# Turned one-hots of the second edge stage: from broadcast rows by DVE instead of by PE and ACT

## What is computed

```python
h = (x_flat @ W_gat).reshape(M, HEADS, NUM_EXPERTS)
...
e = jax.nn.leaky_relu(a_src[src] + a_dst[dst], negative_slope=0.2)
e_max = jax.ops.segment_max(e, dst, num_segments=M)
ee = jnp.exp(e - e_max[dst])
denom = jax.ops.segment_sum(ee, dst, num_segments=M)
...
msg = h[src] * alpha[:, :, None]
agg = jax.ops.segment_sum(msg, dst, num_segments=M)
...
for ei in range(NUM_EXPERTS):
    hh = jax.nn.gelu(x @ W1[ei] + b1[ei], approximate=False)
    out = out + g[..., None] * (hh @ W2[ei] + b2[ei])
```

## Time and profile before

| what | us |
|---|---|
| median of 3 plain runs | 4171.85 (4165.95 to 4173.73) |
| span of the one profiled execution, which is its own time | 5269.4 |
| of it the first edge stage (143.6 to 3096) | 2952.4 |
| of it the second edge stage (3240 to 5127) | 1887.0 |
| PE busy over the span | 3476.8 (66%) |
| DVE busy over the span | 3039.4 (58%) |
| POOL busy over the span | 2649.1 (50%) |
| ACT busy over the span | 1492.7 (28%) |

### The profile page before, as it was taken

One profiled execution on the slowest core, in us unless ns is written; L12 is line 12 of the kernel. 1 busy time (PEld: TensorE's weight loads), 2 busy tenths in 40 slices (PEclk: granted clock), 3 DMA queues, 4 the chain that ended last, 5 costly groups with the idle time before them and its releaser, 6 DMA issues. The chain is left out here.

```text
span 5269.4 us, 87248 instructions
## 1 busy us (share of the span) xinstructions
PE 3476.8 (66%) x16727; PEld 2890.9 (55%) x16728; DVE 3039.4 (58%) x9074; ACT 1492.7 (28%) x4965; POOL 2649.1 (50%) x2767
## 2 busy tenths in 40 slices
PE   5555555665566665666655537888888888888860
PEld 4444444444454444444444436777777777777760
DVE  5566655555565666666666665555555555555558
ACT  3222222222222222222222213333333333333310
POOL 1555555555555555555555522555555555555540
PEclk9777777777777777777777766888888888888865
DMA  5322333332333333333332242111111111111118
GB/s 121 82 78 75 84 82 81 84 84 79 82 82 99 101 101 102 100 101 101 101 84 78 77 79 49 20 20 22 20 20 22 20 20 22 20 21 21 20 16 239
DMA packets 224394, 356.43 MB, mean 68 GB/s; under 512 B 65743, under 2 KB 143761, under 8 KB 224051
## 3 DMA queue, kind: packets, MB, share of 16 engines
q0 software_dynamic: 114560, 234.67, 19.2%
q1 hardware_dynamic: 100624, 109.13, 7.5%
q10 hardware_dynamic: 8867, 9.05, 0.6%
HBM read 294.17 MB, written 45.66 MB: 64 GB/s over the span
## 5 line engine op out<-in xcount | busy, mean ns | idle before, releaser
L791 POOL DMA_INDIRECT msg<-table,idx x1680 | 1630.7, 971 | 1305.1 <-ACT rel L806 844.6
L1466 POOL DMA_INDIRECT xmsg<-xtable,xidx x1060 | 1002.8, 946 | 889.0 <-ACT xidx L1482 589.7
L1159 PE MATMUL psS_e<-msg,hot 128*125 128x260 f32 x3360 | 1182.9, 513 | 281.4 <-issue 162.2
L1159 PEld LDWEIGHTS psS_e<-msg,hot 128*125 128x125 f32 x3360 | 815.5, 254 | 512.3 <-issue 337.3
L888 DVE TENSOR_TENSOR room<-room,psS_e 125x260 f32 x842 | 356.5, 423 | 361.7 <-remote 180.9
L1024 DVE TENSOR_TENSOR msg<-msg,psW_e 128x1024 f32<-128x1024 f32 x420 | 509.5, 1213 | 8.8 <-issue 1.1
L812 ACT CAST hotT<-psT_e 125x512 bf16<-125x512 f32 x422 | 244.7, 580 | 951.6 <-remote 649.7
L1012 DVE TENSOR_REDUCE look<-psD_e 128x32 f32<-128x96 f32 x420 | 106.6, 254 | 700.7 <-remote 553.8
L1076 PE MATMUL psD_e<-ad_b,hotT 125*128 x1684 | 133.9, 182 | 559.8 <-issue 151.3
L1655 PE MATMUL psY<-w,hid 128*125 128x256 f32 x1600 | 457.1, 447 | 56.7 <-issue 29.6
L1065 PEld LDWEIGHTS psT_e<-ident,hot 128*125 128x125 f32 x1692 | 320.7, 240 | 248.2 <-ACT hotT L812 157.7
(11 more groups left out here) (308 smaller groups left out, 4436.9 us busy)
## 6 DMA issues: line engine op xcount, KB each, us to landing
msg<-table,idx POOLq DMA_INDIRECT x1680
experts_out<-y_room SPq DMA_DIRECT2D x101, 224.0 KB
y_back<-experts_out SPq DMA_DIRECT2D x25, 896.0 KB
xmsg<-xtable,xidx POOLq DMA_INDIRECT x1060
xs<-x_all SPq DMA_DIRECT2D x100, 125.0 KB
table<-hrow SPq DMA_DIRECT2D x50, 113.8 KB
x_all<-in_x SPq DMA_DIRECT2D x5, 1120.0 KB
xin<-in_x SPq DMA_DIRECT2D x50, 112.0 KB
```

The source lines that it names most:

```text
L791: nc.gpsimd.indirect_dma_start(msg[:, u, j, :], None, table[:, :], bass.IndirectOffsetOnAxis(ap=idx[:, u, j:j + 1], axis=0)).then_inc(gath ...
L1159: last = nc.tensor.matmul(psS[:, u % 2, j // GT, 0:ROW], hot[:, u, j, :], msg[:, u, j, :], start=j % GT == 0, stop=j % GT == GT - 1)
L1466: nc.gpsimd.indirect_dma_start(msg[:, u, j, :], None, xtable[:, :], bass.IndirectOffsetOnAxis(ap=idx[:, u, j:j + 1], axis=0)).then_inc(gat ...
```

## The change

The turned one-hots are no longer made by PE and ACT. In `nodes`, PE turns the rows of all edges once (eight matmuls with a bfloat16 unit matrix), ACT copies them to SBUF, and one DMA stores them in DRAM as `lo_rows`, a line of 128 numbers for each group. In the second edge stage ACT's `stage`, now four steps ahead, copies the source numbers, copies the rows to float32 (`lo`), adds the class's start to the blocks (`hi_rel`), and issues a DMA that broadcasts the 512 rows of the step to all 128 partitions (`lo_bc`, bfloat16). DVE's `turned_hot` compares them with the partition's number, two steps ahead, and so writes `hotT` in bfloat16. The table of end scores is split once into three bfloat16 parts (`xad_b`); a pick gives 5 times 3 times 8 numbers per edge, and DVE's product and sum work on 480 instead of 160 numbers per partition. DVE's one-hots now read `lo` and `hi_rel`, so `one_hot` and `step` no longer fetch the step's place; the fetch in `add` stays. PE's `turn`, ACT's `keep_turned` and the PSUM tile between them are gone. The diff, cut to its core:

```diff
...
-XAHEAD = 3
+XAHEAD = 4
...
+    lo_rows = nc.dram_tensor("lo_rows", [XEP, P], BF16).ap()
...
     def row(v):
...
+        psL = ps("psL_n", [P, 2, 512])
+        ident_b = sb("ident_b", [P, P], BF16)
+        lo_turned = sb("lo_turned", [P, 2, 512], BF16)
...
+            nc.scalar.copy(ident_b[:], ident[:]).then_inc(ident_kept, 1)
+            for h in range(2):
+                act.wait_ge(los_turned, h + 1)
+                nc.scalar.copy(lo_turned[:, h, :], psL[:, h, :]).then_inc(los_kept, 1)
+            act.wait_ge(los_kept, 2)
+            act.dma_start(lo_rows.rearrange("(c r) e -> r c e", r=P),
+                          lo_turned[:].rearrange("p h (c e) -> p (h c) e", e=P)).then_inc(los_stored, 16)
...
+            act.wait_ge(los_stored, 16)
...
         @block.tensor
         def _(pe):
+            pe.wait_ge(ident_kept, 1)
+            los = lo_all[:].rearrange("p s j -> p (s j)")
+            for h in range(2):
+                for c in range(4):
+                    at = (h * 4 + c) * P
+                    last = nc.tensor.matmul(psL[:, h, c * P:(c + 1) * P], los[:, at:at + P], ident_b[:], start=True,
+                                            stop=True)
+                last.then_inc(los_turned, 1)
             def turn(n):
...
-    CF = CB * 2 * XH
+    XP = 3 * 2 * XH
+    CF = CB * XP
...
+        lo = sb("xlo", [P, XRING, XT])
+        hi_rel = sb("xhi_rel", [P, XRING, XT])
...
-        hotT = sb("xhotT", [NB, 3, XT, P])
+        hotT = sb("xhotT", [NB, 3, XT, P], BF16)
+        xad_b = sb("xad_b", [NB, BLOCKS, 3, 2 * XH], BF16)
+        lo_bc = sb("lo_bc", [P, XRING, XT * P], BF16)
+        rowid = sb("rowid", [P, 1])
...
-        prod = sb("xprod", [P, XT, CB, 2 * XH])
+        prod = sb("xprod", [P, XT, CB, XP])
...
-        psT = ps("psT_g", [NB, 512])
...
+        step_rows = lo_rows.rearrange("(s j) e -> s (j e)", j=XT)
...
         def _(pool):
...
+            nc.gpsimd.iota(rowid[:], [[0, 1]], base=0, channel_multiplier=1,
+                           allow_small_or_imprecise_dtypes=True).then_inc(iotas, 1)
...
             def stage(k, w):
...
-                nc.scalar.copy(idx[:, RING[w], :], xs_i[:, bass.ds(at, 1), :].rearrange("p a j -> p (a j)")) \
-                    .then_inc(staged, 1)
-            def keep_turned(k, w):
-                act.wait_ge(hot_turned, k + 1)
-                nc.scalar.copy(hotT[:, TURN[w], :, :], psT[:, 0:XT * P].rearrange("p (j e) -> p j e", j=XT)) \
-                    .then_inc(hotT_ready, 1)
+                nc.scalar.copy(idx[:, RING[w], :], xs_i[:, bass.ds(at, 1), :].rearrange("p a j -> p (a j)"))
+                nc.scalar.copy(lo[:, RING[w], :], lo_all[:, bass.ds(at, 1), :].rearrange("p a j -> p (a j)"))
+                nc.scalar.activation(hi_rel[:, RING[w], :], hi_all[:, bass.ds(at, 1), :].rearrange("p a j -> p (a j)"),
+                                     ACT.Identity, bias=cls_rel[:, bass.ds(k, 1)]).then_inc(staged, 1)
+                act.dma_start(lo_bc[:, RING[w], :], step_rows[bass.ds(at, 1), :].to_broadcast([P, XT * P])) \
+                    .then_inc(lo_loaded[RING[w]], 16)
...
             def step(k, w):
...
-                if exists(k, 2):
-                    keep_turned(*later(k, w, 2))
...
-            for a in range(2):
-                keep_turned(a, a)
...
         def _(dve):
...
-            dve.wait_ge(iotas, 1)
+            dve.wait_ge(iotas, 2)
...
+            left = prod[0:NB].rearrange("p j b f -> p (j b f)")[:, 0:BLOCKS * 2 * XH] \
+                .rearrange("p (b f) -> p b f", b=BLOCKS)
+            split = Chain(dve, xad_split)
+            split.link(V.tensor_copy(left, xad_all))
+            three_parts(nc, split, left, xad_b)
...
             def one_hot(k, w):
-                at = step_at(dve, k)
-                V.tensor_tensor(hot[:, RING[w], :, :], bcast(node_p, 1, XT),
-                                bcast(lo_all[:, bass.ds(at, 1), :].rearrange("p a j -> p (a j)"), 2, NB),
-                                ALU.is_equal).then_inc(hot_ready, 1)
+                dve.wait_ge(staged, k + 1)
+                V.tensor_tensor(hot[:, RING[w], :, :], bcast(node_p, 1, XT), bcast(lo[:, RING[w], :], 2, NB),
+                                ALU.is_equal)
+            def turned_hot(w, visit):
+                u = RING[w]
+                dve.wait_ge(lo_loaded[u], (visit * RING.count(u) + (w // XRING + 1)) * 16)
+                V.tensor_scalar(hotT[:, TURN[w]].rearrange("p j e -> p (j e)"), lo_bc[0:NB, u, :], rowid[0:NB], None,
+                                ALU.is_equal).then_inc(hotT_ready, 1)
...
             def step(k, w, visit, first):
...
-                at = step_at(dve, k)
...
-                blk = bcast(hi_all[:, bass.ds(at, 1), :].rearrange("p a j -> p (a j)"), 2, CB)
-                first_of = cls_rel[:, bass.ds(k, 1)]
-                ch.also(V.scalar_tensor_tensor(hi[:], blk, first_of, bcast(bid_p, 1, XT), ALU.add, ALU.is_equal))
+                blk = bcast(hi_rel[:, u, :], 2, CB)
+                ch.also(V.tensor_tensor(hi[:], bcast(bid_p, 1, XT), blk, ALU.is_equal))
...
-                ch.link(V.scalar_tensor_tensor(hi_p, blk, first_of, bcast(bid_p, 1, XT), ALU.add, ALU.is_equal))
+                ch.link(V.tensor_tensor(hi_p, bcast(bid_p, 1, XT), blk, ALU.is_equal))
...
-                                bcast(hi[:], 3, 2 * XH), ALU.mult).then_inc(picked_read, 1)
+                                bcast(hi[:], 3, XP), ALU.mult).then_inc(picked_read, 1)
...
-                ch.link(V.reduce_sum(look[:], prod[:].rearrange("p j b f -> p j f b"), AX_X))
+                ch.link(V.reduce_sum(look[:], prod[:].rearrange("p j b (s f) -> p j f (b s)", s=3), AX_X))
...
+                if exists(k, 2):
+                    turned_hot((w + 2) % SPAN, visit + (w + 2) // SPAN)
...
+            for a in range(2):
+                turned_hot(a, 0)
...
-            def turn(k, w):
-                pe.wait_ge(hot_ready, k + 1)
-                if not (isinstance(k, int) and k == 0):
-                    pe.wait_ge(hotT_ready, k)
-                for j in range(XT):
-                    last = nc.tensor.transpose(psT[:, j * P:(j + 1) * P], hot[:, RING[w], j, :], ident[:])
-                last.then_inc(hot_turned, 1)
             def pick(k, w):
...
-                                            xad_all[:, bass.ds(c * CB, CB), :].rearrange("p b f -> p (b f)"),
+                                            xad_b[:, bass.ds(c * CB, CB)].rearrange("p b s f -> p (b s f)"),
...
-            turn(0, 0)
-            turn(1, 1)
+            pe.wait_ge(xad_split, 6)
...
-            turn(2, 2)
...
             def step(k, w, i=None):
...
-                if exists(k, 3):
-                    turn(*later(k, w, 3))
...
```

More of the change, by code:

```diff
@@ L252, in build @@
             nodes(nc, scope, xmix, W_gat, xatt_src, xatt_dst, xtable, x_all, ident, agg, ex_self, xnT, hg_all, xad_all,
-                  row)
+                  lo_all, lo_rows, row)
         acc = sb("acc", [NB, BLOCKS, XROW])
         y_dram = nc.dram_tensor("experts_out", [XE * (BLOCKS // 2) + 1, NB, 2 * D], F32).ap()
-        gating_sums_and_experts(nc, scope, xs_i, lo_all, hi_all, step_i, cls_i, cls_rel, xtable, xad_all, W1, b1, W2, b2, ident, zeros,
+        gating_sums_and_experts(nc, scope, lo_rows, xs_i, lo_all, hi_all, step_i, cls_i, cls_rel, xtable, xad_all, W1, b1, W2, b2, ident, zeros,
                                 node, xnT, acc, y_dram, row)
@@ L1181, in _, with nodes @@
                             step(s, part, first, t, u)
-def nodes(nc, scope, xmix, W_gat, xatt_src, xatt_dst, xtable, x_all, ident, agg, ex_self, xnT_all, hg_all, xad_all, row):
+def nodes(nc, scope, xmix, W_gat, xatt_src, xatt_dst, xtable, x_all, ident, agg, ex_self, xnT_all, hg_all, xad_all,
+          lo_all, lo_rows, row):
     U = 2
@@ L1209, in nodes @@
         psG = ps("psG_n", [NB, U, 512])
+        psL = ps("psL_n", [P, 2, 512])
+        ident_b = sb("ident_b", [P, P], BF16)
+        lo_turned = sb("lo_turned", [P, 2, 512], BF16)
+        ident_kept = sem("ident_kept_n")
+        los_turned = sem("los_turned_n")
+        los_kept = sem("los_kept_n")
+        los_stored = sem("los_stored_n")
         loaded = sem("loaded_n")
@@ L1351, in _, with gating_sums_and_experts @@
                 mm.then_inc(projected, 1)
-def gating_sums_and_experts(nc, scope, xs_i, lo_all, hi_all, step_i, cls_i, cls_rel, xtable, xad_all, W1, b1, W2, b2, ident, zeros, node,
+def gating_sums_and_experts(nc, scope, lo_rows, xs_i, lo_all, hi_all, step_i, cls_i, cls_rel, xtable, xad_all, W1, b1, W2, b2, ident, zeros, node,
                             xnT, acc, y_dram, row):
@@ L1394, in gating_sums_and_experts @@
         iotas_kept = sem("iotas_kept")
+        xad_split = sem("xad_split")
         chain = sem("chain_g")
@@ L1398, in gating_sums_and_experts @@
         gathered = [sem(f"gathered_g{u}") for u in range(XRING)]
-        hot_ready = sem("hot_ready_g")
-        hot_turned = sem("hot_turned_g")
```

(1 more changed line is left out.)

## The result

The changed kernel takes 3974.34 us (median of 4 runs, 3972.2 to 3978.38), the kernel before 4170.0 us beside it: ratio 0.9528, interval 0.9515 to 0.9542. It is faster by 196 us; the forecast was 4120 us, and the result lies under the range (4035 to 4210).

The account below looks back on a forecast made before the run. In the second edge stage PE and DVE's chain were taken as so close that they hold each other up; 4172 + 21 (chain) + 2 (start) - (110 - 35) (waits) = 4120 us, range 4035 to 4210.

Parts of the forecast that it names:

- waits for PE and ACT: Second edge stage, DVE: of 110 us of waits in the plain run, 35 stay, so the time falls by 110 - 35.
- the sum of DVE's chain: Second edge stage, DVE per step: -0.66 - 0.53 + 0.33 + 0.57 + 0.37 = +0.08 us, +21 us over 265 steps.
- the 1497 us: DVE's chain in the second edge stage without its waits: 265 steps of 5.65 us, experts' additions and 25 loop turns included.
- the 110 us of waits: DVE's waits in the plain second edge stage, bracketed between 0 and 110 us; the upper end was taken.
- Fetches, product, sum: DVE per step: two fetches go, -0.66 - 0.53 us; product grows to 480 elements, +0.33; strided sum grows, +0.57.
- The compare: DVE's new 512-element compare: 0.45 us long from one-source rows, adding 0.37 us a step (0.21 to 0.60).
- DVE was the bound already: Rival, second edge stage: only 60 us of waits in the plain run, 35 staying, time 4170 us; chance 0.15.
- More waits in the plain run: Rival, second edge stage: half of the profiled 390 us, 195, is in the plain run, time 4035 us; chance 0.14.
- PE falls by 309 us (forecast 313): PE, second edge stage: without turning and with bfloat16 picks, work drops by 313 to 1119 us, under DVE's chain.
- not under 0.74: Sign of the clock rival: PE's granted clock under 0.74 makes PE the bound again; at 0.70, 4200 us; chance 0.07.
- ACT's late Exp: ACT ahead of DVE's weighing: two one-hots, about 1 us, cover the Exp; without that cover DVE waits up to 0.6 us.
- the compare waits for POOL: Rival, DVE's compare: it waits until POOL's running gather ends, 0.36 us a step, 95 us, time 4215 us; chance 0.13.

## Why the prediction was wrong

The direction was right, the mechanism and the size were not: -52 us forecast, -196 us measured. The forecast let DVE's chain grow a little and took its whole gain, 75 us, from waits for PE and ACT, because "PE and DVE's chain are so close that they must hold each other up". The runs show the reverse: the waits gave 24 us, and DVE's own order the rest. So the direction came out right partly by luck. The step that failed is the sum of DVE's chain, "+0.08 us a step", which measured -0.38, together with the 25 turns of the loop that were left inside the 1497 us as something that stays, and the 110 us of waits.

| term | forecast | measured | from |
|---|---|---|---|
| fetches, us a step | -1.19 | -1.22 | 6.00 - 4.78, fetches put back |
| form and reading place of the one-hots, us a step | 0 | -0.33 | 6.33 - 6.00, no staging against fetches put back |
| product, us a step | +0.33 | +0.33 | 0.36 to 0.69, start to start |
| sum, us a step | +0.57 | +0.58 | 0.47 to 1.05 |
| compare, us a step | +0.37 | +0.26 | its start to the next one's |
| together, times 265, us | +21 | -101 | 4.78 - 5.16 |
| turn of the loop, us | 0 | -73 | 24 times (4.13 - 0.79) - (0.47 - 0.18) |
| waits for PE and ACT, us | -75 | -24 | 58.6 to 34.5 |
| start, us | +2 | not told apart | |
| sum, us | -52 | -198 | |

*Fetches, product, sum.* Right to 0.03 us each; all three were read from single rows of the same kind.

*The other operands.* The prediction counted instructions that vanish and instructions that grow, and passed over two that only change their form: the one-hots of blocks lost the scalar that hangs on the step and a source at a fetched place (0.234 us in L1558 above, 0.172 in L1596), and the register work for their addresses went too. That is -0.33 us a step, 87 us, and the largest miss. Of it 0.19 us come with the class's start when the fetches are there (0.10 without them) and 0.14 with the reading place. The two instructions' own lengths make up 0.12 us; that the rest is register work is argued, not shown.

*The loop's turn.* Its gap was in the trace of before; it was never read, because only ordinary steps were. Taking the fetches' instructions out of the loop removed it, about 73 us. Not the fetch as such does it: covered, the two fetches cost no time in a step, and the gap was there.

*The compare.* Taken at 0.45 us from the one-source rows, it takes 0.345 us undisturbed. That is 29 us of the miss. Written in float32 it takes 0.478 us (median of the run with float32 picks), less than the 0.60 us that was the sign there of a length hanging on bfloat16 at both ends, and 0.133 us more than in bfloat16. The Trainium skill, "VectorE: DVE Perf Modes", section "The perf-mode tier table", gives four elements a cycle for bfloat16 and two for float32; the estimate from it, 0.29 us, was nearer to the 0.345 us than the 0.45 us taken. The compare into float32 reads bfloat16, a mix that the table doesn't list.

*The waits.* Taken at the upper end of their bracket, 110 us, because PE's rows came close to it; they were 58.6 us, and 34.5 stay. The rival "DVE was the bound already" had put 60 and 35 there, and was right on that; its time failed with the same chain. "More waits in the plain run" came nearest in time with the wrong mechanism.

*PE, ACT, DMA, clock.* PE falls by 309 us (forecast 313), near it partly by luck: the groups of the turning and the picks fell by 369 us, and the experts' second products took 53 us more. The granted clock is 0.90, not under 0.74, no DVE group waits for the broadcast rows, which land in 3.1 us, and ACT's late Exp costs 2.7 us. The errors that lowered the time (compare 29, form 87, loop 73 us) and the one that raised it (waits 51 us) don't cancel.

## What to carry to other kernels

When numbers move from a register-addressed table to a staged tile, count three things on the engine that is relieved: the exposed fetch, the form of every instruction that used the number, and the length of its loop. Look at the step where a loop turns as closely as at an ordinary one: a gap there that goes with the instruction packets was paid on 23 of 24 turns here. And try each part of a change alone, since here a part that costs 279 us by itself and one that gives 190 us by itself together gave 196.

## What the runs showed of the hardware

The strided sum of 480 numbers is 0.358 us quicker when they lie in PSUM (0.658 against 1.016 us). Before that run it was only a guess from the shorter sums of the earlier trace rows.

The rival "the compare waits for POOL" exists in small. In the changed kernel the compare takes 342 to 589 ns; over 1.2 times its median in 53 of 265 cases, 9.4 us together (9.9 us with a few smaller ones). These are all the compares that began 0.47 to 0.65 us after a gather's start, and no others. The later such a one began, the less it lost (589 ns from 0.471 us on, 420 ns from 0.649 us on), so that all of them ended 1.06 to 1.07 us after the gather's start, as if held up to one and the same moment of the gather. DVE and POOL in order of time:

```profile
2998.49 0.68 DVE L1567 TENSOR_TENSOR xhot<-psK,xlo 128x500 f32<-128x500 f32 x1
2998.60 0.95 POOL L1501 DMA_INDIRECT xmsg<-xtable,xidx  x1 [0.30 <-issue]
2999.09 0.57 DVE L1573 TENSOR_SCALAR xhotT<-lo_bc,rowid 125x512 bf16<-125x512 bf16 x1
```

The compare began 0.49 us into the gather. The two-source one-hot ahead of it is never longer than 680 ns (median 679), and the gather isn't pushed (943 ns before, 947 after). The Trainium skill, "SBUF — State Buffer", section "Who interferes with whom", speaks of a lock for whole instructions; the trace has one that holds for a part of the gather, 0.24 us at most, and costs 9.9 us instead of the 95 us of that rival.
